# A deformable convolution with routed experts: the four hat spreads as row groups of one array pass, a band ahead of sampling

## The chip, the cores and the metric

One core of a Trainium2 chip runs the whole kernel. The metric is device time in microseconds (us) of one execution, smaller is better. TensorE (PE) multiplies matrices, VectorE (DVE), ScalarE (ACT) and GpSimd (POOL) work element by element, SyncE (SP) issues transfers.

## What is computed

The input is four images of 32 x 32 positions with 128 channels. First a deformable 3 x 3 convolution is added to it, then a top-2 mixture of eight experts:

```python
x = x + _L0_conv_ref(_ln_c(x), w_offset, b_offset, filt)
t = _to_tokens(x)
t = t + _L0_ffn_ref(_ln_t(t), gate_w, gate_b, W1, b1, W2, b2)
# in the convolution, for each position and each of nine taps:
sampled = (v00*(1-dy)*(1-dx) + v01*(1-dy)*dx + v10*dy*(1-dx) + v11*dy*dx) * mask
# in the experts, for each token:
probs = softmax(xf @ gate_w + gate_b); top2_vals, top2_idx = top_k(probs, 2)
out = sum over the two chosen e of top2_vals * (gelu(xf @ W1[e] + b1[e]) @ W2[e] + b2[e])
```

The offsets and the mask of every tap come from an ordinary 3 x 3 convolution of the layer-normalised input.

## The kernel before

The 4096 positions are 32 bands of 128 (four image rows; eight tiles of 4 x 4). Three stages follow each other: the offset convolution for all images (to about 43 us), the band loop (about 50 to 250 us), and the experts on 39 blocks of 256 routed rows (from about 262 us), at whose end results are gathered and added.

In the band loop sampling is a matrix product. For each tile a window of 10 x 10 positions (`xwin`, 100 partitions) is multiplied with a weight matrix `S` of 100 x (9 taps x 16 positions). `S` is the product of a y part and an x part, each a "hat" (one minus the distance, cut at zero) for ten window rows or columns. Per band:

- POOL computes `dist` (`distances`, L570), DVE makes `tent` and `hat` of it (`hats`, L904 to L912), ACT writes its bf16 high part (`hi_part`, L715), POOL the middle and low parts (`split`, L579 to L582), so that `hat3` holds three bf16 parts that sum to the f32 value. A tap takes 60 columns (three parts of 20), a pair of taps 120.
- PE transposes `hat3` pair by pair into bank 4 (`transpose_hats`, five matmuls, L1269), ACT evacuates it to `hatT` (`evacuate_hatT`, L721): 120 rows of 5 x 128 columns.
- PE spreads y and x onto the 100 window cells (`spread_hats`, L1279 y, L1282 x). The constant `spread_sb` has ones where row and cell belong together; a unit u is 512, 512 or 128 columns (`UNITS`: taps 0, 2, 4, 6, then 1, 3, 5, 7, then 8). Each matmul contracts all 120 rows, those of the other tap and axis against zeros. y goes to bank 0 or 1, x to bank 2 or 3.
- ACT copies y (`copy_y`, L729 into `ysp`), DVE multiplies it with x from PSUM into `S` (`multiply`, L923).
- PE samples in three groups of 3, 3 and 2 tiles (`sample`, L1315), ACT evacuates each (`evacuate_samples`, L758 into `samp`), PE projects with the nine filter taps (`project`, L1326, five taps and then four).
- DVE adds the residual and takes statistics (`residual`, L931 to L939), ACT the square root (`std_band`, L765), DVE normalises (`normalise`, L945 and L949 into `xn2`). PE transposes (`transpose_tokens`, L1336), ACT evacuates (L770), PE multiplies with the gate (`gate`, L1340), DVE takes the two largest (`choose`, six links, L960 to L982), PE counts how many tokens of each expert stand before each (`count_places`, L1347 and L1348 into bank 7), DVE turns that into rows (`place_rows`, four links, L991 to L1007).
- POOL copies the normalised band twice into `payload` with its destination (`pack`, L591 and L593) and scatters it by two indirect transfers (`scatter`, L602).

Each engine runs its own list of these calls in a fixed order, `step(b, ...)`, called by `band_loop`: four bands written out, then a loop of four bands a turn, then the rest. Semaphores alone tie the lists together. In step b PE's list is: spread 0 of b, counts of b-3, spread 1 of b, five taps of the projection of b-1 (after `samples_ready(b-1)`), token transpose of b-2, spread 2 of b, four taps, gate of b-2, sample group 0 of b, hat transposes of b+1, sample groups 1 and 2. ACT's: two y copies, tokens, third y copy, samples 0, hatT of b+1, std of b-1, samples 1, high part of b+2, samples 2. DVE's: places of b-3 between the three multiplies of b, then residual of b-1, choose of b-2 and hats of b+2 link by link, then normalise of b-1. POOL's: split of b+2, distances of b+3, scatter of b-3, pack of b-2. `transpose_hats` also waits until the logits of band b-3 have been read from bank 4, `project` until the places of an earlier band have been read from bank 7. Two slots (`par`, b % 2) exist of most tiles.

Before the loop stand band 0's hats and spreads, and a flag `far` (L1030) on which every engine branches (L1352 on PE): offsets above 2 would take a slower gather. After the loop come a count matmul (L1416), the plan of blocks (L1146 to L1167), eight padding writes into `routed` (L366), and the first row load (L496), which waits for scatters and padding.

## Time and profile before

| | |
|---|---|
| median of 3 runs | 403.73 us (402.92 to 405.21) |
| profiled execution | span 400.1 us from the first to the last instruction; its own total is not given |
| PE busy | 315.2 us, 79% of the span |
| PE weight loads | 264.9 us, 66% |
| DVE busy | 227.3 us, 57% |
| ACT busy | 195.6 us, 49% |
| POOL busy | 228.9 us, 57% |
| mean granted TensorE clock | 0.926 |

The span is shorter than a run's time, since start and end of the program lie around it. An engine's busy share is a mean over three stages with different limits, so the loop is to be read by itself: by stage, by what each engine waits for there, and by one band laid out in time. In such a layout the difference of two starts on PE is what an instruction costs the engine, while its shown duration also holds the time until its result is out.

### The profile page before, as it was taken

The page shows a single profiled execution, that of the slowest core. Times are in us where ns is not written, and L with a number is a line of the kernel's source. Part 1 is how long each engine was busy: PE and PEld are TensorE (multiplying, and loading weights), DVE is VectorE, ACT ScalarE, POOL GpSimd, SP SyncE. Part 2 cuts the span into 40 slices and gives each one's busy share as a digit, 9 for nine tenths or more (in the row PEclk, how much of TensorE's full clock was granted, in tenths as well). Part 3 has the DMA queues.
Part 4 walks back from the last instruction along what each step waited for, and adds up shares of the span by engine and source line. Part 5 has one row for each costly group of instructions (what it writes and reads, how often), then busy time and mean ns, then how long its engine had stood idle before and what let it go on. Part 6 is the DMA issues. An engine that isn't in the chain of part 4 may idle for free.

```text
span 400.1 us, 9901 instructions
## 1 busy us (share of the span) xinstructions
PE 315.2 (79%) x2395; PEld 264.9 (66%) x2395; DVE 227.3 (57%) x988; ACT 195.6 (49%) x526; POOL 228.9 (57%) x351
## 2 busy tenths in 40 slices
PE   0999799999999999999999995049989797885000
PEld 0354688888889888898898994038867686774000
DVE  3983257878778787787887876502222122332085
ACT  1253566565565665756656652314444444442063
POOL 4013043777777777777777766204777777777300
PEclk9999899999999999999999999558999999999555
DMA  8958612222222222222222220855777777762298
GB/s 209 274 164 249 265 54 75 89 80 100 78 93 85 82 99 78 90 94 76 98 84 83 95 80 26 145 139 169 223 222 243 230 231 232 227 221 72 82 315 234
DMA packets 52450, 57.88 MB, mean 145 GB/s; under 512 B 6892, under 2 KB 40423, under 8 KB 52424
## 3 DMA queue, kind: packets, MB, share of 16 engines
q1 hardware_dynamic: 45031, 48.16, 39.1%
q0 software_dynamic: 4544, 8.44, 6.6%
q10 hardware_dynamic: 2848, 0.99, 1.4%
q8 instruction: 9, 0.15, 0.2%
q14 instruction: 18, 0.14, 0.1%
HBM read 30.70 MB, written 14.97 MB: 114 GB/s over the span
## 4 chain that ended last, share of the span: by engine, by line
PE 53%; SPq 16%; issue 10%; DMA 6%; ACT 4%; DVE 4%; POOL 2%; ACTq 2%; DVEq 1%; POOLq 0%
PE bank L1326 18%; PE bank L1315 15%; SPq L481 5%; PE bank L1248 5%; SPq L490 4%; SPq L496 3%; DMA wide<-result 2%; PE bank L1279 2%; PE bank L1433 2%; ACT samp L758 2%; PE bank L1269 2%; PE bank L1260 2%; POOL result L658 2%; DMA routed<-padding_sb 1%; DMA result<-y,to 1%
## 5 line engine op out<-in xcount | busy, mean ns | idle before, releaser
L658 POOL DMA_INDIRECT result<-y,to x78 | 76.8, 985 | 43.8 <-DVE to L1191 26.8
L1326 PE MATMUL bank<-filt_sb,samp 128*128 128x128 f32 x576 | 79.3, 283 | 4.1 <-ACT samp L758 2.5
L1326 PEld LDWEIGHTS bank<-filt_sb,samp 128*128 128x128 f32 x576 | 69.1, 191 | 18.1 <-ACT samp L758 14.2
L1315 PE MATMUL bank<-S,xwin 100*128 100x144 f32 x512 | 78.9, 298 | 1.8 <-issue 1.7
L602 POOL DMA_INDIRECT routed<-payload,slot x64 | 63.2, 987 | 18.5 <-issue 13.5
L758 ACT ACTIVATE samp<-bank 128x432 f32<-128x432 f32 (+1 forms) x96 | 46.3, 484 | 52.8 <-PE bank L1315 52.8
L1315 PEld LDWEIGHTS bank<-S,xwin 100*128 100x128 f32 x512 | 67.7, 193 | 2.2 <-issue 2.0
L923 DVE TENSOR_TENSOR S<-ysp,bank 100x512 f32<-100x512 f32 (+1 forms) x96 | 52.5, 550 | 22.9 <-ACT ysp L729 21.8
L1433 PE MATMUL bank<-rowsT,w_blk 128*128 128x256 f32 x156 | 44.4, 408 | 13.3 <-DMA w_blk<-w_all 10.2
L1199 DVE TENSOR_TENSOR y<-bank,w_blk 128x256 f32<-128x256 f32 x39 | 16.6, 425 | 66.0 <-PE bank L1442 64.2
L822 ACT ACTIVATE rowsT<-bank 128x256 f32<-128x256 f32 x39 | 15.0, 384 | 61.0 <-PE bank L1424 61.0
L729 ACT ACTIVATE ysp<-bank 100x512 f32<-100x512 f32 (+1 forms) x96 | 43.6, 494 | 2.4 <-PE bank L1279 1.5
L579 POOL TENSOR_TENSOR rest<-hat 128x180 f32<-128x180 f32 x32 | 17.0, 531 | 47.2 <-ACT hat L715 47.2
L1442 PE MATMUL bank<-w_blk,hid 128*128 128x128 f32 x312 | 42.1, 279 | 0.0
L1433 PEld LDWEIGHTS bank<-rowsT,w_blk 128*128 128x128 f32 x156 | 27.5, 197 | 20.0 <-ACT hid L829 8.0
L1442 PEld LDWEIGHTS bank<-w_blk,hid 128*128 128x128 f32 x312 | 38.8, 195 | 0.3 <-ACT hid L829 0.2
L829 ACT ACTIVATE hid<-bank,w_blk 128x256 f32<-128x256 f32 x78 | 32.6, 473 | 0.6 <-PE bank L1433 0.6
L1279 PE MATMUL bank<-hatT,spread_sb 120*100 120x512 bf16 (+1 forms) x96 | 32.0, 333 | 0.1
L1282 PE MATMUL bank<-hatT,spread_sb 120*100 120x512 bf16 (+1 forms) x96 | 31.2, 325 | 0.8 <-DVE S L923 0.8
L1424 PE MATMUL bank<-ident_sb,rows_in 128*128 128x128 f32 x78 | 15.9, 287 | 15.1 <-DMA rows_in<-routed 15.1
L570 POOL TENSOR_TENSOR dist<-offs,rel_sb 128x180 f32<-128x180 f32 x32 | 16.2, 508 | 19.3 <-issue 10.7
L1424 PEld LDWEIGHTS bank<-ident_sb,rows_in 128*128 128x128 f32 x78 | 11.0, 147 | 20.3 <-DMA rows_in<-routed 15.1
(110 smaller groups left out, 493.1 us busy)
## 6 DMA issues: line engine op xcount, KB each, us to landing
w_blk<-w_all SPq DMA_DIRECT2D x39, 321.0 KB
xwin<-lines SPq DMA_DIRECT2D x64, 120.0 KB
xwin<-lines SPq DMA_DIRECT2D x32, 160.0 KB
rows_in<-routed SPq DMA_DIRECT2D x39, 129.0 KB
wide<-result SPq DMA_DIRECT2D x16, 256.0 KB, 4.8
w_all<-in_experts SPq DMA_DIRECT2D x4, 642.0 KB, 7.4
out_tiles<-res SPq DMA_DIRECT2D x8, 256.0 KB, 4.6
wide<-in_x_rows SPq DMA_DIRECT2D x3, 512.0 KB, 8.6
```

The source lines that it names most:

```text
L602: nc.gpsimd.indirect_dma_start(routed, bass.IndirectOffsetOnAxis(slot[:, par, c2:c2 + 1], 0), payload[:, par, c2, :], None).then_inc((s.sc ...
L658: nc.gpsimd.indirect_dma_start(result, bass.IndirectOffsetOnAxis(to[:, slot, j:j + 1].bitcast(U32), 0), y[:, slot, j, :], None, bounds_che ...
L729: nc.scalar.activation(ysp[:, slot, 0:n], bank[slot][0:Q, 0:n], ACT.Copy).then_inc(s.y_ready, 1)
L758: nc.scalar.activation(sample_view(par, g), bank[5 + (par + g) % 2][:, 0:GROUPS[g] * TAPS * TT].rearrange("c (t k p) -> c t k p", k=TAPS, ...
L829: nc.scalar.activation(hid[:, slot, h, :], bank[RING + slot][:, h * BLOCK:(h + 1) * BLOCK], ACT.Gelu, bias=w_blk[:, slot, HID + h:HID + h ...
L923: nc.vector.tensor_tensor(S[:, par, c0:c0 + n], ysp[:, slot, 0:n], bank[2 + slot][0:Q, 0:n], ALU.mult).then_inc(s.S_ready, 1)
L1279: nc.tensor.matmul(bank[slot][0:Q, 0:n], spread_sb[:, 2 * odd, :], moving, start=True, stop=True).then_inc(s.y_psum, 1)
L1282: nc.tensor.matmul(bank[2 + slot][0:Q, 0:n], spread_sb[:, 2 * odd + 1, :], moving, start=True, stop=True).then_inc(s.x_psum, 1)
L1315: last = nc.tensor.matmul(bank[5 + (par + g) % 2][:, i * TAPS * TT:(i + 1) * TAPS * TT], xwin[:, par, t, :], weights[:, t], start=True, st ...
L1326: last = nc.tensor.matmul(bank[7][:, 0:C], samp[:, par, j, :], filt_sb[:, order[j], :], start=(j == 0), stop=(j == TAPS - 1))
L1433: last = nc.tensor.matmul(bank[RING + slot][:, h * BLOCK:(h + 1) * BLOCK], w_blk[:, slot, h * P:(h + 1) * P], rowsT[:, slot, :], start=Tru ...
L1442: last = nc.tensor.matmul(bank[slot][:, BLOCK + j * C:BLOCK + (j + 1) * C], hid[:, slot, h, j * P:(j + 1) * P], w_blk[:, slot, W_UP + h * ...
```

## The change

- `hat3` gets groups of 32 columns: for each tap and each axis (y, x) three parts of ten and two zeros. A pair of taps is 128 columns, so `hatT` has four row groups: y and x of the even tap, y and x of the odd tap. The constant `spread` is 128 x 100.
- A spread contracts the 30 rows of one group (`spread_taps`). `spread_hats` issues four in a row: y and x of unit 0 and y and x of unit 1, into banks 0 to 3. `spread_last` issues y and x of unit 2 later, when the first banks have been read.
- The spreads of band b+1 are issued in step b, ahead of the samples of b, the last unit behind them, and hat transposes of b+2 at the end. Copies and multiplies move along.
- POOL computes distances four bands ahead, first in its step, then scatters band b-4, then stamps, then splits b+3. DVE's `normalise` writes both copies of the payload itself, into one of four (`QUEUED`) slots, waiting for an older scatter; POOL's `stamp` adds the destination. `transpose_tokens` reads the payload. `xn2` is gone.
- The places are counted into bank 4 from column 384 on (`WHERE`), between sample groups 0 and 1. `project` no longer waits for them; `transpose_hats` does, for an older band.
- Before the loop band 1's transposes and evacuation, band 2's hats and high part, and distances up to band 3 are done ahead of or around the flag. The tail is reordered.

```diff
-            def spread_hats(b, par, u):
-                pe.wait_ge(s.hatT_ready, b + 1)
-                slot, n, odd = (par + u) % 2, UNITS[u], u % 2
-                moving = hatT[:, 4, :] if u == 2 else hatT[:, 0:4, :].rearrange("r i t -> r (i t)")
-                at_least(pe, s.y_ready, b * 3 + u - 1)
-                nc.tensor.matmul(bank[slot][0:Q, 0:n], spread_sb[:, 2 * odd, :], moving,
-                at_least(pe, s.S_ready, b * 3 + u - 1)
-                nc.tensor.matmul(bank[2 + slot][0:Q, 0:n], spread_sb[:, 2 * odd + 1, :], moving,
+            def spread_taps(par, u):
+                slot, n, odd = (par + u) % 2, UNITS[u], u % 2
+                for yx, arrived in ((0, s.y_psum), (1, s.x_psum)):
+                    first = GROUP * (2 * odd + yx)
+                    rows = slice(first, first + PARTS * WIN)
+                    moving = hatT[rows, 4, :] if u == 2 else hatT[rows, 0:4, :].rearrange("r i t -> r (i t)")
+                    nc.tensor.matmul(bank[2 * yx + slot][0:Q, 0:n], spread_sb[rows, :], moving,
+                                     start=True, stop=True).then_inc(arrived, 1)
+            def spread_hats(b, par):
+                pe.wait_ge(s.hatT_ready, b + 1)
+                at_least(pe, s.y_ready, b * 3)
+                at_least(pe, s.S_ready, b * 3)
+                spread_taps(par, 0)
+                spread_taps(par, 1)
+            def spread_last(b, par):
+                pe.wait_ge(s.y_ready, b * 3 + 1)
+                pe.wait_ge(s.S_ready, b * 3 + 1)
+                spread_taps(par, 2)
...
 PE, step b
-                        spread_hats(b, par, 0)
-                        count_places(b - 3, 1 - par)
-                        spread_hats(b, par, 1)
                         samples_ready(b - 1)
                         project(b - 1, 1 - par, range(FIRST_TAPS), ORDER)
+                        pe.wait_ge(s.hatT_ready, b + 2 if not known or b + 2 < BANDS else BANDS)
+                        transpose_tokens(b - 2, (q + 2) % QUEUED)
-                        transpose_tokens(b - 2, par)
-                        spread_hats(b, par, 2)
                         project(b - 1, 1 - par, range(FIRST_TAPS, TAPS), ORDER)
                         gate(b - 2, par)
+                        spread_hats(b + 1, 1 - par)
                     sample(b, par, loads, 0)
-                        transpose_hats(b + 1, 1 - par)
+                        pe.wait_ge(s.route, (b - 2) * 6 + 1)
+                        count_places(b - 3, 1 - par)
                     sample(b, par, loads, 1)
                     sample(b, par, loads, 2)
+                        spread_last(b + 1, 1 - par)
+                        transpose_hats(b + 2, par)
...
 ACT, step b
-                        copy_y(b, par, 0)
-                        copy_y(b, par, 1)
                         evacuate_tokens(b - 2, par)
-                        copy_y(b, par, 2)
+                        copy_y(b + 1, 1 - par, 0)
+                        copy_y(b + 1, 1 - par, 1)
                     evacuate_samples(b, par, 0)
-                        evacuate_hatT(b + 1)
                         std_band(b - 1, 1 - par)
                     evacuate_samples(b, par, 1)
-                        hi_part(b + 2, par)
                     evacuate_samples(b, par, 2)
+                        evacuate_hatT(b + 2)
+                        copy_y(b + 1, 1 - par, 2)
+                        hi_part(b + 3, 1 - par)
...
 POOL, step b
-                        split(b + 2, par)
-                        distances(b + 3, 1 - par)
-                        scatter(b - 3, 1 - par)
-                        pack(b - 2, par)
+                        distances(b + 4, par)
+                        scatter(b - 4, par, q)
+                        stamp(b - 2, (q + 2) % QUEUED)
+                        split(b + 3, 1 - par)
...
 DVE, step b, new order
+                    place_rows(b - 4, par, 1)
+                    hats(b + 3, other, 0)
+                    place_rows(b - 4, par, 2)
+                    hats(b + 3, other, 1)
+                    place_rows(b - 4, par, 3)
+                    hats(b + 3, other, 2)
+                        multiply(b, par, 2)
+                    residual(b - 1, other, 0)
+                    choose(b - 2, par, 0)
+                    residual(b - 1, other, 1)
+                    choose(b - 2, par, 1)
+                    residual(b - 1, other, 2)
+                    choose(b - 2, par, 2)
+                    place_rows(b - 3, other, 0)
+                        multiply(b + 1, other, 0)
+                    choose(b - 2, par, 3)
+                    choose(b - 2, par, 4)
+                        multiply(b + 1, other, 1)
+                    choose(b - 2, par, 5)
+                    normalise(b - 1, other, (q + 3) % QUEUED)
...
 DVE, normalise
-                at_least(dve, s.payload_ready, 2 * (b - 1))
-                nc.vector.tensor_scalar(xn2[:, par, :], x1[:, b, :], mv1[:, par, 0:1], rs1[:, par:par + 1],
+                if not isinstance(b, int) or b >= QUEUED:
+                    dve.wait_ge((s.scat_even, s.scat_odd)[par],
+                                (b // 2 - 1) * 32 if isinstance(b, int) else (b - par) * 16 - 32)
+                nc.vector.tensor_scalar(payload[:, q, :, 0:C], x1[:, b, :].unsqueeze(1).broadcast_to([P, 2, C]),
+                                        mv1[:, par, 0:1], rs1[:, par:par + 1],
```

## Rows read from the trace of the kernel before

**Rows 1.** The page's chain that ended last: share of the span by engine.
```profile
PE 53%; SPq 16%; issue 10%; DMA 6%; ACT 4%; DVE 4%; POOL 2%; ACTq 2%; DVEq 1%; POOLq 0%
```

**Rows 2.** Busy time by stage: us, PE, PEld, DVE, ACT, POOL, PEclk, DMA, GB/s.
```profile
94.00:119.00 25.00, 24.43 (x202) 21.39 (x200) 19.87 (x93) 15.48 (x42) 18.42 (x33) 1.00 0.26 88
```

**Rows 3.** Waits from 94 to 243 us: waiter, released by: total us, times, longest.
```profile
POOL rest L579 <- ACT hat L715: 24.0, 23, 1.1
DVE S L923 <- ACT ysp L729: 15.7, 24, 0.7
```

**Rows 4.** Timeline of PE over one band: start us, duration us, line, tiles, count.
```profile
150.28 1.38 PE L1326 MATMUL bank<-filt_sb,samp 128*128 128x128 f32 x10
151.49 0.27 PE L1336 MATMUL bank<-ident_sb,xn 128*128 128x128 f32 x1
151.60 0.22 PE L1279 MATMUL bank<-hatT,spread_sb 120*100 120x128 bf16 x1
...
151.72 1.11 PE L1326 MATMUL bank<-filt_sb,samp 128*128 128x128 f32 x8
152.66 0.29 PE L1340 MATMUL bank<-gw_sb,xn2T 128*128 128x8 f32 x2
152.81 0.98 PE L1315 MATMUL bank<-S,xwin 100*128 100x144 f32 x6
153.62 0.44 PE L1269 MATMUL bank<-identb_sb,hat 128*120 128x128 bf16 x5
153.91 1.44 PE L1315 MATMUL bank<-S,xwin 100*128 100x144 f32 x10
155.19 0.38 PE L1279 MATMUL bank<-hatT,spread_sb 120*100 120x512 bf16 x1
...
155.62 0.17 PE L1347 MATMUL bank<-both,before_sb 128*128 128x8 bf16 x1
...
155.68 0.40 PE L1279 MATMUL bank<-hatT,spread_sb 120*100 120x512 bf16 x1
...
156.46 1.38 PE L1326 MATMUL bank<-filt_sb,samp 128*128 128x128 f32 x10 [0.17 <-ACT samp L758]
```

**Rows 5.** Timeline of ACT in the same band.
```profile
150.12 1.08 ACT L729 ACTIVATE ysp<-bank 100x512 f32<-100x512 f32 x2
...
153.88 0.53 ACT L758 ACTIVATE samp<-bank 128x432 f32<-128x432 f32 x1 [1.64 <-PE bank L1315]
...
156.00 0.40 ACT L758 ACTIVATE samp<-bank 128x288 f32<-128x288 f32 x1
```

**Rows 6.** Timeline of PE and its weight loads around the second offset convolution.
```profile
21.53 0.27 PE L1260 MATMUL bank<-fold_sb,conv_sb 128*128 128x27 f32 x1
21.73 0.64 PE L1248 MATMUL bank<-xnT,woff_sb 128*32 128x512 f32 x4
22.19 0.13 PEld L1248 LDWEIGHTS bank<-xnT,woff_sb 128*32 128x32 f32 x4 [0.30 <-issue]
22.62 0.13 PEld L1248 LDWEIGHTS bank<-xnT,woff_sb 128*32 128x32 f32 x4 [0.30 <-issue]
...
25.63 0.60 PE L1248 MATMUL bank<-xnT,woff_sb 128*32 128x512 f32 x2
26.16 0.14 PEld L1236 LDWEIGHTS bank<-ident_sb,wide 128*128 128x128 f32 x1 [0.84 <-issue]
```

**Rows 7.** Timeline at both ends of the band loop.
```profile
45.52 1.28 ACT L777 ACT_TABLE_LOAD   x1
...
51.88 1.38 PE L1326 MATMUL bank<-filt_sb,samp 128*128 128x128 f32 x10
...
241.71 2.27 PE L1326 MATMUL bank<-filt_sb,samp 128*128 128x128 f32 x18
```

**Rows 8.** The chain behind the loop, in order of time: start us, us, what.
```profile
256.13 5.79 DMA routed<-padding_sb
```

**Rows 9.** Timeline of POOL: the last scatter.
```profile
252.89 0.96 POOL L602 DMA_INDIRECT routed<-payload,slot  x1 [0.30 <-issue]
```

More of the change, by code:

```diff
@@ L611, in _ @@
             split(1, 1)
+            distances(2, 0)
+            split(2, 0)
+            distances(3, 1)
             pool.wait_ge(s.offs_ready, IMAGES)
@@ L1028, in _ @@
                 multiply(0, 0, u)
+            for link in range(3):
+                hats(2, 0, link)
             dve.wait_ge(s.near_psum, 1)
@@ L1122, in _ @@
                 b = BANDS - 1
[L1123 removed]
+                run(place_rows, b - 3, 0, range(1, 4))
+                residual(b, 1, 0)
                 choose(b - 1, 0, 0)
[L1125 to L1129 removed]
+                residual(b, 1, 1)
+                choose(b - 1, 0, 1)
```

209 lines of the change are left out of this document (104 added, 105 removed).

## The prediction

> **What bounds the kernel now.** I read the page's chain of work first: PE holds 53% of the whole span [rows 1]. The change touches only the band loop (32 bands, from about 50 us to 244 us), so I then took busy time by stage: in 25 us of that loop PE is busy 24.43 us at a granted clock of 1.00, VectorE (DVE) 19.87, POOL 18.42, ACT 15.48 [rows 2]. A band takes 6.18 us: the ten matmuls that open a projection start at 150.28 and again at 156.46 [rows 4]. The waits say how far the others are from mattering: POOL idles 24.0/23 = 1.04 us a band for ACT's hat, DVE 15.7/24 = 0.65 us for ACT's ysp [rows 3]. Last I read one band of PE instruction by instruction, from start to start [rows 4]: projection 1.21, token transpose 0.11, two small spreads 0.12, rest of projection 0.94, gate 0.15, sample group 0 0.81, hat transposes 0.29, sample groups 1 and 2 1.28, big y and x spread 0.43, counts 0.06, big y and x spread 0.43. Sum 5.83. The remaining 0.35 is a stall: PE has nothing from about 156.11 to 156.46, because ACT evacuates the last sample group only at 156.00, for 0.40 us [rows 5]. So a band is PE's work plus the tail of one ACT evacuation.
>
> **The change part by part.**
>
> *Four spreads side by side.* Each big spread streams 512 columns and costs 0.21 to 0.22 us of issue; four in a row are 0.86 [rows 4]. Now each contracts 30 rows in its own group of 32 rows, writing its own bank. The trace has no matmul split by rows, but it has four split by output columns: the offset convolution. There a round of four, each 512 columns in two passes, comes every 22.62 - 22.19 = 0.43 us [rows 6], which is the streaming time of one. So four together at the price of one is shown for columns; I take it for rows. Bounds of the pack: 0.22 (all start at once) to 0.86 (no overlap). What stands in between is the weight loads: each of the four needs its own 100 columns, and a hat transpose, 0.29/5 = 0.058 us, holds one load and one 128-column stream, so a load is at most 0.058, likely 0.04. Three of them ahead of the last stream: 0.22 + 3 x 0.04 = 0.34. I take 0.34.
>
> *Entering and leaving the split array.* Going into the split, the convolution's first start is 0.20 behind the last fold matmul's start (21.53 to 21.73), where otherwise 0.11 separates two such small ones: +0.09. Coming out, the last two convolution matmuls start at 25.63 and stream 0.43, to 26.06; the next weights load only starts at 26.16, with none hidden beneath the stream: +0.10 and a load of 0.04 [rows 6]. So 0.10 in, 0.13 out; bounds 0 (rows may behave otherwise than columns) and 0.2 each. The Trainium skill, "TensorEngine Tiling (Array Packing)", Key Properties, says that changing the tiling mode drains TensorE while changing only the tile doesn't; by that rule the new order pays four times a band, and these rows agree with 0.1 us. The skill's "TensorE: Matmul & The Clock Gate", Part 3, gives 3.07x for four row tiles of K=32 and 512 columns; by it the pack would be an estimated 0.28 us, and the band 0.06 shorter than mine.
>
> *Order on PE.* Between gate and sample group 0 now stand in, pack and out: 0.10 + 0.34 + 0.13 = 0.57. Behind sample group 2 stand the two small spreads (in 0.10, work 0.14, out 0.13) and the five transposes 0.29, together 0.66. Sample group 2 reaches the projection no sooner than 0.26 (ACT started at 153.88, PE's issue of group 0 had ended at 153.62) + 0.40 + 0.06 = 0.72 [rows 4, 5]. So all of that 0.66 is hidden by the evacuation and costs nothing; if ACT's part fell away it would cost 0.66. Sum of the new band: 1.21 + 0.11 + 0.94 + 0.15 + 0.57 + 0.81 + 0.06 + 1.28 + 0.72 = **5.85 us**, 0.33 less than 6.18.
>
> *ACT.* Its order must let the sample evacuations go at once. Two ysp copies take 1.08 [rows 5], from about 0.5 behind the pack's start, so they end 1.6 behind it; group 0 is ready at 0.34 + 0.13 + 0.81 + 0.26 = 1.54. Level, and the short std behind it has half a us before group 1. ACT doesn't bind, by a small margin. Hat evacuation, third ysp copy and hi part now come behind the samples, under the next projection.
>
> *VectorE.* It loses nothing and writes the normalised row twice (256 elements in place of 128). Its 4.91 us a band (19.87/25 x 6.18) becomes 5.05; the steps that now follow each other directly on it (residual, statistics; chosen, both; placed, slot) wait for their own predecessor, +0.2 to +0.5. There is a ring through it: gate, pack, group 0, counts (0.10 + 0.34 + 0.13 + 0.81), then places, three multiplies, rest of choose, normalise, placing and hats, and only then may PE start the next spreads. Taking away residual, statistics and the first choose steps, which lie ahead of the places (about 1.2), leaves 5.05 + 0.4 - 1.2 + 0.2 for the count to land = 4.45, plus 1.38: **5.8**. This is just below PE's 5.85.
>
> *POOL.* It loses the 256-element payload copy and keeps distances, three splits, two scatters and the stamp. It idled 1.04 us a band for ACT [rows 3], so everything it does now, gaps included, is 6.18 - 1.04 = 5.14: under 5.85 even before the copy goes. The new order puts distances and the scatters of the band four back ahead of the split; the split is not late for it, since its hi part comes later too. The new DVE wait for a scatter looks at one issued a whole band earlier: covered.
>
> *Places in bank 4.* The projection no longer waits for the place step; in its stead hat transposes wait for one that is a band older. In the band shown neither held PE up (the projection's releaser is ACT), so nothing is gained, and nothing lost while the counts run between groups 0 and 1: were they late, all of group 1 would be.
>
> *Before the loop.* Hats of band 2 (three DVE steps, about 1.0) now precede the far flag on which every engine branches, and ACT has one more hat evacuation and a hi part, some 1 us, ahead of the 1.28 us table load of 45.52 [rows 7]. That delays the first samples by 1.0 to 2; the spreads of band 1, 0.86, and its copies no longer lie behind sample 0. Net +0.3 (bounds -0.6, +1.5).
>
> *After the loop.* Band 30's slot is written behind band 31's choice, so the last scatters end up to 2 us later. They are covered: the first row load waits for padding writes whose last one lands at 256.13 + 5.79 = 261.92, and the last scatter's issue ended at 253.85, 8 us earlier [rows 8, 9]. The last normalise comes some 0.5 earlier, the padding rows 0.35 later: -0.1.
>
> **Sum.** From the first projection (51.88) to the last (241.71) are 189.8 us for 31 bands [rows 7], the first two and the last shorter since they lack token work or spreads. New: first 5.6, last 5.3, 29 x 5.85 = 169.7, together 180.6: -9.2. With +0.3 and -0.1: -9.0. The profiled execution shows no total of its own but its span, 400.1; the runs' median of 403.73 is 3.6 above it, kept. 403.7 - 9.0 = **394.7 us**.
>
> **Rivals.**
> - *Rows pack cheaply and no drain is seen.* Pack 0.22 to 0.28, switches 0: band 5.5 to 5.6, DVE's ring 5.45. 29 x 5.55 + 10.6 = 171.5: 385.5. For it: switches inside one stream of bf16 may differ from conv's. Against: both edges of every convolution show the gap.
> - *VectorE's ring becomes the bound.* If its self-waits cost 0.2 more than I took, the band is 6.0: 399. For it: 5.85 against 5.8, and no slack. It shows as PE waiting for S before the pack.
> - *Slower: rows don't overlap.* Pack 0.86 with its drains 1.09 between gate and samples, against 0.57: band 6.37; 29 x 6.37 + 11.2 = 195.9, so +6.1 + 0.2: 410. It decides where pack plus drains pass 0.90. For it: no row of the trace has such matmuls. Against: the column split does overlap.
> - *Nothing gained*: an order of waits (ysp copies late, so every sample evacuation late) puts back the 0.33: 403.
>
> **Chances.** Forecast (392 to 397) 0.45, cheap pack 0.17, VectorE's ring 0.20, nothing gained 0.07, slower 0.11. Leaving out the slower case and the far end of the cheap one gives 385 to 404. A measurement here tells about 0.5% (2 us) from no change: faster 0.81, same 0.08, slower 0.11.
>
> **What would show it.** Band starts of the projection 5.85 apart; the four big spread rows starting within 0.15 us; PE weights of sample group 0 starting some 0.1 behind the pack with idle time on PEld; a stall at the projection, still released by ACT's last sample evacuation, of under 0.1. If PE instead waits for DVE ahead of the spreads, the ring has it. The prediction is wrong at its root if the four starts are 0.2 apart, or if sample evacuations start more than 0.3 behind PE's issue.

## The result, and the profile after

The changed kernel runs in 400.37 us (median of 4 runs, 397.23 to 401.61), the kernel before in 403.62 beside it: a ratio of 0.9897, with a 95% interval of 0.9851 to 0.9944. Timed again beside a part of the experiments it gave 397.97 against 403.54, or 0.9854 (0.9825 to 0.9883). The experiments are compared with that second timing. They ran on three chips, on which the kernel before had medians from 403.54 to 404.21, and the changed kernel was timed again on one of them; so between chips it is the ratios that compare, and 0.001 is 0.4 us. The change gained 3.3 us in the first timing and 5.6 in the second, where 9.0 were forecast. The time of 400.37 lies outside the forecast's 392 to 397 and inside the wide range of 385 to 404; of the gain little more than a third came in the first timing and three fifths in the second.

The loop did nearly what was predicted; what was lost lies at its two ends. First the busy time by stage of the changed kernel, with the columns and length of [rows 2]:

```profile
144.00:169.00 25.00, 24.80 (x215) 21.82 (x213) 21.69 (x100) 17.43 (x44) 17.43 (x31) 1.00 0.27 93
```

PE went from 24.43 to 24.80 busy in 25 us, so the stall of [rows 4] is nearly gone. DVE went from 19.87 to 21.69, which is 21.69/25 x 5.84 = 5.07 us a band (5.05 predicted).

One band on PE, laid out in time, which answers to [rows 4]:

```profile
149.97 1.38 PE L1357 MATMUL bank<-filt_sb,samp 128*128 128x128 f32 x10
151.19 0.27 PE L1367 MATMUL bank<-ident_sb,payload 128*128 128x128 f32 x1
151.30 1.06 PE L1357 MATMUL bank<-filt_sb,samp 128*128 128x128 f32 x8
152.19 0.29 PE L1371 MATMUL bank<-gw_sb,xn2T 128*128 128x8 f32 x2
152.41 0.42 PE L1299 MATMUL bank<-hatT,spread_sb 30*100 30x512 bf16 x4
152.76 1.00 PE L1347 MATMUL bank<-S,xwin 100*128 100x144 f32 x6
153.60 0.17 PE L1378 MATMUL bank<-both,before_sb 128*128 128x8 bf16 x1
...
153.66 1.59 PE L1347 MATMUL bank<-S,xwin 100*128 100x144 f32 x10
155.18 0.26 PE L1299 MATMUL bank<-hatT,spread_sb 30*100 30x128 bf16 x2
155.37 0.45 PE L1287 MATMUL bank<-identb_sb,hat 128*128 128x128 bf16 x5
155.81 0.38 PE L1357 MATMUL bank<-filt_sb,samp 128*128 128x128 f32 x1
```

The projection (line 1357) starts at 149.97 and 155.81: 5.84 us a band, with 5.85 predicted. Most bands of the loop take 5.75 to 5.89; three take 6.05 to 6.97, and they come up below. The four big spreads (line 1299) occupy one row of 0.42. Per term, start to start: gate and the way in 0.22, pack and the way out 0.35, group 0 0.84, counts 0.06, groups 1 and 2 with the way into the small spreads 1.52, small spreads 0.19, transposes 0.44.

The waits from 94 to 243 us, which answer to [rows 3] (waiter, releaser, total, times, longest):

```profile
DVE x L932 <- PE bank L1357: 13.6, 26, 2.3
PEld bank L1347 <- issue: 7.3, 24, 1.4
PEld bank L1357 <- ACT samp L757: 2.9, 18, 0.2
PE bank L1347 <- DMA xwin<-lines: 1.6, 3, 1.1
```

DVE no longer waits for ysp but for the projection, 13.6/26 = 0.52 us: it has slack. PE's loader waits for the sample evacuation 0.16 at a time. The last line is new: in three places PE waits for a window transfer, 1.6 us in all, and these are the three long bands.

Now the ends. Before's last fold matmuls and its first two projections, then after's:

```profile
40.77 1.92 PE L1260 MATMUL bank<-fold_sb,conv_sb 128*128 128x27 f32 x16
...
57.42 0.82 PE L1326 MATMUL bank<-filt_sb,samp 128*128 128x128 f32 x5
```

```profile
41.73 1.92 PE L1276 MATMUL bank<-fold_sb,conv_sb 128*128 128x27 f32 x16
...
45.71 0.34 PE L1299 MATMUL bank<-hatT,spread_sb 30*100 30x128 bf16 x2 [1.71 <-DVE S L924]
...
49.96 4.21 PE L1347 MATMUL bank<-S,xwin 100*128 100x144 f32 x16
...
55.22 3.95 PE L1357 MATMUL bank<-filt_sb,samp 128*128 128x128 f32 x18
...
59.45 2.41 PE L1347 MATMUL bank<-S,xwin 100*128 100x144 f32 x16
...
62.37 0.82 PE L1357 MATMUL bank<-filt_sb,samp 128*128 128x128 f32 x5
```

Before: the fold ends at 42.69, projection 0 starts at 51.88 [rows 7], projection 1 at 57.42. After: 43.65, 55.22 and 62.37. The 16 sampling matmuls of band 0 take 4.21 us where band 1's take 2.41, and projection 0 takes 3.95 where [rows 7] has 2.27 for the same 18 at the loop's end. The busy time in stretches of 2 us says why (the columns of [rows 2]; the granted clock is third from the end), before first:

```profile
46.00:48.00 2.00, 1.05 (x6) 1.08 (x7) 0.00 (x0) 1.00 (x2) 0.00 (x0) 0.84 0.27 107
48.00:50.00 2.00, 2.00 (x13) 1.98 (x12) 0.00 (x0) 1.24 (x2) 0.41 (x1) 0.50 0.00 0
50.00:52.00 2.00, 2.00 (x11) 1.47 (x11) 0.95 (x3) 1.35 (x4) 0.49 (x2) 0.81 0.06 16
```

```profile
44.00:46.00 2.00, 0.29 (x3) 0.20 (x4) 1.90 (x6) 1.08 (x2) 0.00 (x0) 0.79 0.95 388
46.00:48.00 2.00, 0.97 (x15) 0.67 (x13) 1.40 (x6) 1.37 (x4) 0.00 (x0) 0.50 0.17 67
48.00:50.00 2.00, 0.64 (x5) 0.23 (x5) 0.00 (x0) 1.93 (x5) 1.88 (x4) 0.50 0.02 4
...
56.00:58.00 2.00, 2.00 (x11) 2.00 (x11) 0.29 (x1) 0.58 (x3) 1.27 (x3) 0.50 0.22 70
58.00:60.00 2.00, 2.00 (x15) 1.65 (x15) 0.58 (x2) 0.45 (x1) 0.71 (x2) 0.79 0.21 82
```

Both kernels lose the clock in the head. Before, it falls within the stretch from 46 to 48, is at its lower level (1.2 of 2.4 GHz, shown as 0.50) from 48 to 50 and is back at about 51: some 3.4 us at the lower level, an estimate from the clock of these stretches. After, it falls within 44 to 46, where PE was busy for 0.29 of 2 us, PE is busy for 0.97 and 0.64 in the two stretches behind, and the clock stays at 0.50 until nearly 59: an estimated 13.7 us.

Last, the chain behind the loop, to be read against [rows 8]:

```profile
245.33 2.28 DMA routed<-payload,slot
247.71 0.41 DVE slot L1010
...
253.58 6.66 DMA routed<-padding_sb
```

A scatter now stands ahead of the last write of `slot`, and the padding writes behind it. The whole difference of the two profiled executions, by marks on PE (the last mark is the first matmul on routed rows, 264.49 before and 262.80 after):

| stretch | predicted | measured |
|---|---|---|
| start to end of fold | 0 | +1.0 |
| end of fold to second projection | +0.4 | +4.0 (14.73 to 18.72) |
| second to last projection, 30 bands | -9.3 | -8.4 (184.29 to 175.85) |
| last projection to first routed rows | -0.1 | +1.8 (22.78 to 24.58) |
| rest | 0 | -0.4 |
| sum | -9.0 | -2.1, from 400.1 to 398.0 |

The table compares two single executions, and the one of the kernel before was a quick one. In every timed execution the total is 1.8 to 1.9 us above the span (here 399.82 and 398.0), so the span of 400.1 stands for a total of about 402.0, an estimate, while the lowest of all timed executions of the kernel before is 402.38 and its median 403.62. The stretches that it shows for the kernel before may thus be up to some 1.7 us shorter than usual together; where, isn't known. Its mean clock, 0.926, is near the upper end of the timed executions (0.916 to 0.930).

The first line is not the change's: the end of fold varied from 42.1 to 44.0 over the experiments that start from the changed kernel, with equal code up to there. Measured from the end of the fold, the second projection of the second timing's profile stands at 61.69 - 43.25 = 18.44, and this distance is used below.

### The profile page after: what moved, and what is told of

It reads as the page before. It is cut to its first block, busy times and chain, and to the rows that moved or that the text cites. A ratio compares the mean times of both kernels' runs of the same rounds, so it can differ in the third digit from the quotient of the medians.

```text
span 398.0 us, 9795 instructions
## 1 busy us (share of the span) xinstructions
PE 310.6 (78%) x2395; PEld 259.8 (65%) x2395; DVE 229.8 (58%) x988; ACT 202.8 (51%) x526; POOL 218.1 (55%) x319
## 4 chain that ended last, share of the span: by engine, by line
PE 55%; DMA 17%; SPq 16%; issue 6%; DVE 2%; POOL 1%; ACT 1%; ACTq 1%; POOLq 0%; DVEq 0%
PE bank L1347 18%; PE bank L1357 15%; DMA xwin<-lines 6%; PE bank L1264 5%; SPq L482 5%; DMA w_blk<-w_all 4%; PE bank L1299 4%; PE bank L1468 3%; SPq L491 3%; SPq L497 3%; PE bank L1287 2%; DMA wide<-result 2%; PE bank L1477 2%; PE bank L1276 2%; DMA fold_sb<-in_fold 2%
## 5 line engine op out<-in xcount | busy, mean ns | idle before, releaser
L1347 PE MATMUL bank<-S,xwin 100*128 100x144 f32 x512 | 80.8, 308 | 1.6 <-DMA xwin<-lines 1.6
L1357 PE MATMUL bank<-filt_sb,samp 128*128 128x128 f32 x576 | 77.8, 285 | 1.1 <-issue 1.0
L1347 PEld LDWEIGHTS bank<-S,xwin 100*128 100x128 f32 x512 | 69.5, 194 | 11.0 <-issue 9.1
L1357 PEld LDWEIGHTS bank<-filt_sb,samp 128*128 128x128 f32 x576 | 70.9, 196 | 5.6 <-ACT samp L757 3.6
L1468 PE MATMUL bank<-rowsT,w_blk 128*128 128x256 f32 x156 | 44.2, 407 | 14.9 <-DMA w_blk<-w_all 13.7
L757 ACT ACTIVATE samp<-bank 128x432 f32<-128x432 f32 (+1 forms) x96 | 47.1, 491 | 10.6 <-PE bank L1347 6.5
L1299 PE MATMUL bank<-hatT,spread_sb 30*100 30x512 bf16 (+1 forms) x192 | 22.2, 366 | 4.4 <-issue 2.7
L1459 PEld LDWEIGHTS bank<-ident_sb,rows_in 128*128 128x128 f32 x78 | 11.1, 147 | 22.1 <-DMA rows_in<-routed 17.7
L720 ACT ACTIVATE hatT<-bank 128x640 bf16<-128x640 bf16 x32 | 22.5, 704 | 4.6 <-PE bank L1287 2.4
```

The costliest lines, as they stand in the source:

```text
L757: nc.scalar.activation(sample_view(par, g), bank[5 + (par + g) % 2][:, 0:GROUPS[g] * TAPS * TT].rearrange("c (t k p) -> c t k p", k=TAPS, ...
L1299: nc.tensor.matmul(bank[2 * yx + slot][0:Q, 0:n], spread_sb[rows, :], moving, start=True, stop=True).then_inc(arrived, 1)
L1347: last = nc.tensor.matmul(bank[5 + (par + g) % 2][:, i * TAPS * TT:(i + 1) * TAPS * TT], xwin[:, par, t, :], weights[:, t], start=True, st ...
L1357: last = nc.tensor.matmul(bank[7][:, 0:C], samp[:, par, j, :], filt_sb[:, order[j], :], start=(j == 0), stop=(j == TAPS - 1))
L1459: last = nc.tensor.transpose(bank[slot][:, j * P:(j + 1) * P], rows_in[:, slot, j, 0:C], ident_sb[:, :])
L1468: last = nc.tensor.matmul(bank[RING + slot][:, h * BLOCK:(h + 1) * BLOCK], w_blk[:, slot, h * P:(h + 1) * P], rowsT[:, slot, :], start=Tru ...
```

## The experiments

Two questions: was the loop's gain what I took it for (rows packed, stall hidden), and what took 4 us ahead of it and 1.8 behind it.

### All 128 rows, no packing

```diff
-                    moving = hatT[rows, 4, :] if u == 2 ...
-                    nc.tensor.matmul(bank[2 * yx + slot][0:Q, 0:n], spread_sb[rows, :], moving,
+                    moving = hatT[:, 4, :] if u == 2 ...
+                    nc.tensor.matmul(bank[2 * yx + slot][0:Q, 0:n], spread_sb[:, at:at + Q], moving,
```

> The changed kernel with every spread contracting all 128 rows again (its weights zero outside its group of 32), so no two can run side by side and the array is never split; order and waits are those of the change. Theory (the loop's gain comes from packing, four for 0.35 us in place of 0.86 plus switches): the step from the first spread to sample group 0 becomes 0.86, the band 5.84 + 0.86 - 0.35 - 0.07 = 6.28 at most, 6.14 if PE alone sets it; total 8 to 12 us above the changed kernel, thus above the kernel before. Rival (the gain comes from moving the spreads out of the stretch between sampling and projection, and packing matters little): band under 6.0, total within 4 us of the changed kernel.

408.71 us, ratio 1.0121 (1.0093 to 1.015): 10.7 over the changed kernel, as expected, and slower than the kernel before.

```profile
150.59 1.04 PE L1301 MATMUL bank<-hatT,spread_sb 128*100 128x512 bf16 x4 [0.17 <-issue]
151.46 0.90 PE L1349 MATMUL bank<-S,xwin 100*128 100x144 f32 x6
```

The four spreads hold PE 151.46 - 150.59 = 0.87 against 0.35, and a band, from gate to gate (150.13 to 156.46), is 6.33 (6.23 in the mean of 30 bands). All that the order gains is less than what four spreads cost when they no longer hide behind an evacuation: the packing carries the gain.

### The kernel before with row groups alone, y and x as a pair

```diff
-SLOT = PARTS * HATS
+GROUP = 32
+SLOT = 2 * GROUP
...
-                nc.tensor.matmul(bank[slot][0:Q, 0:n], spread_sb[:, 2 * odd, :], moving,
+                for yx, arrived in ((0, s.y_psum), (1, s.x_psum)):
+                    nc.tensor.matmul(bank[2 * yx + slot][0:Q, 0:n], spread_sb[rows, :], moving,
```

> The kernel before with the row groups alone: y and x of a unit side by side (three packs of two a band), its order, waits and payload copies untouched. Theory (each entry into a split array costs 0.1 and each way out 0.13, about what a pack of two saves): big packs 0.26 + 0.23 against 0.43, the small one 0.12 + 0.23 against 0.12, of which the stall of 0.35 ahead of the projection hides the two big ones: band 6.2 to 6.35, total 0 to 5 us above the kernel before. Rival (switching is nearly free for rows): band under 6.1 only if the stall moves too; PE's stall grows by 0.3 and the total stays within 1 us.

413.77, ratio 1.0247 (1.0219 to 1.0275).

```profile
156.34 0.42 PE L1283 MATMUL bank<-hatT,spread_sb 30*100 30x512 bf16 x2
156.69 0.18 PE L1348 MATMUL bank<-both,before_sb 128*128 128x8 bf16 x1
...
157.46 0.71 PE L1327 MATMUL bank<-filt_sb,samp 128*128 128x128 f32 x4 [0.23 <-ACT samp L758]
```

A pair costs 156.69 - 156.34 = 0.35, as much as the pack of four, against 0.43 unsplit, and it is paid twice; between the projection's two halves the small pair takes 0.19, where [rows 4] has 0.12 for both. The sign was expected, the size was not: +10 us. The band of 6.34 that is shown here is the shortest of every four in the loop; the others take 6.57 to 6.66, and from the second projection to the last a band takes 193.68/30 = 6.46 us in the mean, against 184.29/30 = 6.14 before. Most of that is waiting ahead of the projection. From 94 to 243 us:

```profile
PE bank L1327 <- ACT samp L758: 6.3, 16, 0.5
PE bank L1327 <- DVE place L991: 2.7, 5, 0.5
```

PE waits 6.3 + 2.7 = 9.0 us there, and the kernel before 1.8 + 1.1 = 2.9 for the same two: a quarter of a microsecond a band more. In the band shown the two big pairs save 0.08 each, but the small one gives 0.07 back, and what stands ahead of each pair takes longer to the next start (token transpose 0.20 for 0.11, rest of the projection 1.00 for 0.94, sample groups 1 and 2 1.38 for 1.28). So row groups alone, in the old places, lose, by the changes of mode and by a longer stall. Why the stall grows was not followed up, and pairs in the new order were not run: this doesn't show that two at a time can never pay.

### The small spreads back over full rows

```diff
+                    if u == 2:
+                        rows = slice(0, 2 * SLOT)
```

> The changed kernel with the two small spreads behind the samples over all 128 rows (no split of the array there; weights zero outside their group), the four big ones packed as before. The prediction put the two switches of this place (0.23 us) at nothing, since the last sample evacuation covers them: total within 0.7 us of the changed kernel, the stall ahead of the projection 0.1 to 0.2 longer. Rival (they are on the path): 0.1 to 0.2 a band, 3 to 6 us lower.

397.22, ratio 0.9828 (0.9794 to 0.9862), against the changed kernel's 0.9854: the two intervals overlap.

```profile
150.63 1.38 PE L1361 MATMUL bank<-filt_sb,samp 128*128 128x128 f32 x10
...
156.47 0.71 PE L1361 MATMUL bank<-filt_sb,samp 128*128 128x128 f32 x4 [0.17 <-ACT samp L758]
```

The band stays at 5.84 (5.97 in one of four), the wait for ACT returns (0.17): the two changes of mode behind the samples lie under the evacuation, as the sum had them.

### One more VectorE copy a band

```diff
+                    nc.vector.tensor_copy(gsum[:, 0:4, :], filt_sb[:, 0:4, :])
                     normalise(b - 1, other, (q + 3) % QUEUED)
```

> The changed kernel with one more VectorE instruction a band, a copy of 512 elements into a tile nobody uses, ahead of normalise: 0.3 to 0.6 us of VectorE time. The prediction's ring through VectorE was 5.8 us against PE's 5.85: by it the band grows by the copy less 0.05, and the total by 8 to 16 us. Rival (the ring was overpriced: VectorE still waits 13.6/26 = 0.52 us a band for the projection in the changed kernel): the wait shrinks by the copy, the band stays below 5.95, total within 3 us.

406.54, ratio 1.0058 (1.0034 to 1.0082), about 8 us over the changed kernel by the ratios, within what was expected.

```profile
150.90 0.42 PE L1300 MATMUL bank<-hatT,spread_sb 30*100 30x512 bf16 x4 [0.44 <-issue]
```

The band (gate at 150.17 and 156.43) grows by 0.42, what the copy takes: PE waits 0.44 ahead of the pack. That holds for three bands of four in the loop (6.19 to 6.33); the fourth stays at 5.84. So the ring through VectorE is real, and in three bands of four it is within some hundredths of PE's own period; in the fourth it has at least 0.4 to spare.

### Window transfers cut to 3/10 (a part of the windows isn't loaded, so part of the sampling is left out)

```diff
+                    if not isinstance(b, int) or b >= 2:
+                        w1 = w0 + 1
```

> The changed kernel with each window load from band 2 on cut to one window column of its part (3 of 10 columns, so 120 KB a band in place of 400 KB; stale data stand in the rest, so that part of the sampling is left out). Theory (the windows now land just at the time they are needed, and three or four times in the loop later): the PE waits for windows (1.6 us in the trace of the changed kernel) vanish, every band 5.84, total 1.5 us lower. Rival 1 (transfers held the bands up all through): bands fall below 5.80 and the total by over 3 us. Rival 2: nothing moves.

397.83, ratio 0.9837 (0.9816 to 0.9858), against 0.9854. The wait of PE for `xwin` is gone from the list, no band between the second and the last projection takes over 5.84, and the 30 bands take 174.2 us in place of 175.5 and 175.9 in the two profiles of the changed kernel. The transfers take 7.3 to 8.2 us each where they stand on the chain. So the windows cost 1.3 to 1.7 us of the loop in the traces; the total moved by 0.7, which the intervals don't tell from nothing, nor from the 1.5 that were expected.

### Four places for the slots

```diff
-            slot = sb("slot", [P, 2, 2], U32)
+            slot = sb("slot", [P, QUEUED, 2], U32)
```

> The changed kernel with four places for the slot numbers in place of two, and in the four bands of the tail a wait for the scatter two bands older. Theory (behind the loop VectorE's last slot write waits 0.98 us for a scatter's landing, and the padding rows are queued behind it on VectorE): that wait is gone, the padding writes start 1 us earlier and the first row block arrives 1 us earlier: 1.0 us below the changed kernel. Rival (the padding writes then share the DMA queues with the last scatters and land later, as they took 6.66 us here against 5.79 before): under 0.4 us gained.

398.04, ratio 0.9855 (0.9831 to 0.988).

```profile
250.15 7.06 DMA routed<-padding_sb
```

The scatter is gone from the chain, but the last padding write took 7.06 us to land, 6.66 in the changed kernel's profile and 5.79 before. The total shows no gain. The tail itself, from the last projection to the first matmul on routed rows, does: it is 22.9 to 23.5 us in the six profiles with four places for the slots (they follow below) and 23.8 to 24.6 in eight with two, the changed kernel's own two among them. So the wait was real and worth under a microsecond; the other half of the tail's 1.8 is the landing, in which padding writes and late scatters are under way together. Whether these scatters slow it was not tested.

### The far flag earlier

```diff
             spread_hats(0, 0)
+            (near counts of the flag)
             spread_last(0, 0)
             transpose_hats(1, 1)
...
+            (flag)
             for u in range(3):
                 multiply(0, 0, u)
```

> The changed kernel with the far flag written ahead of band 0's multiplies and band 2's hats (as early as the near counts allow), ScalarE's masks and table load ahead of the extra hat evacuation, all else the same. Theory A (the gain was lost ahead of the loop, because every engine branches on a flag that now comes 2 us later and VectorE needs 4.8 us from the flag to its first loop step, 47.64 to 52.39): flag near 45.5, first projection near 53.1 in place of 55.12, total 2 us below the changed kernel (about 398.3). Rival B (the flag is not what the first projection waits for; the half TensorE clock between 46 and 59 us is): first projection and total stay within 0.7 us of the changed kernel.

398.27, ratio 0.9833 (0.9802 to 0.9864). The flag came at 45.21 in place of 47.50, but the first projection at 54.65 and not at 53.1, and of the expected 2 us the ratio shows less than 1, within the intervals:

```profile
49.34 0.67 PE L1299 MATMUL bank<-hatT,spread_sb 30*100 30x512 bf16 x4 [2.62 <-ACT hatT L720]
...
54.65 2.27 PE L1357 MATMUL bank<-filt_sb,samp 128*128 128x128 f32 x18
```

In this kernel ACT's evacuation of band 1's hats had come behind the table load of [rows 7], so the wait for the flag became a wait for that. Yet projection 0 ran in 2.27: here the clock had fallen later, within 46 to 48, and was back at 54. From the fold's end it is 16.7 to projection 1, not 18.4. That the median doesn't follow says how much one profiled start differs from the next.

### Idle matmuls ahead of the loop

```diff
+            for _ in range(3):
+                nc.tensor.matmul(bank[7][:, :], ident_sb[:, :], filt_sb[:, 0:4, :]..., start=True, stop=True)
...
+            for _ in range(5): (the same, after transpose_hats(1, 1))
```

> The changed kernel with eight idle f32 matmuls of 512 columns on PE ahead of the loop (three behind the first spreads, five behind the near counts) into a bank not yet in use, so that PE isn't idle there; the flag stays late. Theory: the granted clock stays at 1.00 where it was 0.50 from 46 to 59 us, so samples 0 (4.14 us at the low clock, about 2.4 at the full one) and projection 0 (3.74 against 2.2) give back 1.5 to 3 us of the first bands; the second projection starts near 60 in place of 62.44. Rival: VectorE's late entry into the loop sets the first band and the clock costs nothing (within 0.5 us of the changed kernel), or the filler delays the near counts and the flag and it is slower by up to 1 us.

397.13, ratio 0.9822 (0.9802 to 0.9841).

```profile
46.20 4.56 PE L1340 MATMUL bank<-filt_sb,ident_sb 128*128 128x512 f32 x10
51.04 2.41 PE L1354 MATMUL bank<-S,xwin 100*128 100x144 f32 x16
...
54.61 2.23 PE L1364 MATMUL bank<-filt_sb,samp 128*128 128x128 f32 x18
```

The granted clock is 1.00 in every stretch from 46 to 60, and samples and projection take 2.41 and 2.23. But the row itself was too long, 4.56 us: the loop's first pack starts 50.69 - 42.30 = 8.4 behind the fold's end, in the changed kernel 49.36 - 43.65 = 5.7, and the second projection 60.03 - 42.30 = 17.7, not 18.4. A part of what the clock gave back went there. By the ratios the total is 1.3 us lower, and the intervals overlap; the pair of kernels at the end of this section is the one that prices the clock.

### Flag, idle matmuls and slots together

> The changed kernel with the early flag, the idle matmuls ahead of the loop and the four slot places together. If the three losses at the ends are separate, the gains add up: flag 2.1, clock 3.2, tail 2.3 by the first looks, 5 to 7 us below the changed kernel (393.5 to 395.5), 0.975 of the kernel before. If flag and clock are one loss seen twice (filling the wait or shortening it), 3.5 to 5 us.

396.28, ratio 0.9818 (0.979 to 0.9847): no more than the idle matmuls gave, within the intervals, where 3.5 to 7 us below the changed kernel were expected and 1.7 came. Projection 0 starts at 54.63 again.

### Another order at the head, with and without idle matmuls

Flag early, evacuation of band 1's hats ahead of the masks, distances of band 3 ahead of the split, four slots; 3 + 1 idle matmuls, and none.

> The changed kernel with all causes of the late first band treated at once: far flag first, ScalarE evacuates band 1's hats ahead of masks and table load (in the early-flag run PE waited for just this evacuation, queued behind the table load), POOL computes distances of band 3 ahead of the split of band 2 (VectorE's first loop step waited for them there), idle matmuls only as long as the gap (1.3 us and 0.9 us, since those of the run before were 4.5 us long by themselves), and the four slot places. Theory (the head's loss is a chain of several queues, each of which takes over when one is removed): first projection at 52 to 53 in place of 54.6, second near 57.8 to 58.5 in place of 60.1; total 1.5 to 3 us below the run with all three single remedies (396.3). Rival (VectorE's own way from the flag into the loop, 4.8 us, sets it): first projection stays above 54.

> The same as the run with the rearranged head, without the idle matmuls. Theory (the low clock costs by itself): the granted clock falls to 0.50 near 46 us, samples 0 take 4.1 us in place of 2.4, and the first projection comes 1 to 1.7 us later than with them; total 1 to 2 us higher. Rival (VectorE's entry into the loop hides it): equal within 0.5 us.

398.93, ratio 0.9881 (0.9857 to 0.9905), and 397.49, ratio 0.9854 (0.983 to 0.9877). Both missed. With idle matmuls the flag stood behind them (47.17 in place of 44.70), VectorE entered the loop at 53.73, PE was busy for 0.76 and 0.56 in the stretches 52 to 54 and 54 to 56, and the clock fell to 0.50 all the same. Without them VectorE entered at 51.60, 6.9 behind a flag at 44.70. So the flag was not what held it.

### Masks first; then all repairs, with and without idle matmuls

```diff
             copy_y(0, 0, 0)
             copy_y(0, 0, 1)
+            for m in range(1, IMAGES):
+                mask_image(m)
             copy_y(0, 0, 2)
...
             distances(2, 0)
+            distances(3, 1)
             split(2, 0)
```

> The changed kernel with one move ahead of the loop: ScalarE's three remaining image masks come before its copies of the hats, and the distances of band 3 before the split of band 2. Theory (VectorE enters its loop about 4 us after the last image mask, and the first placing, and so the first loading of projections, hangs on it): VectorE's first loop step starts at 49.5 to 50.5 instead of 52.4; TensorE's first projection starts at 54 to 54.6 instead of 55.2, because the samples of band 0 at a granted clock of 0.50 end there anyway; total 0.3 to 1 us under the changed kernel's 398, at 397 to 397.7. Rival (the entry hangs on the far flag, not on the masks): VectorE's first step stays at 51.5 or later, time unchanged.

> All the repairs together: image masks first, far flag early, distances of band 3 early, a short row of idle matmuls (two of 512 float32 columns) ahead of the loop, four slot places. Theory (the head lost 3 to 5 us to late masks and to a granted clock of 0.50 in bands 0 and 1): VectorE's first step at about 49.3, first projection at 52 to 53 and 2.2 us long, second at 57.5 to 58.5; total 393.5 to 395. Rival (the first projection is held by the samples of band 0 and their evacuation, whatever comes before): first projection at 54 or later, total 396 to 397, as the kernel with flag, idle matmuls and slots.

> The same without the idle matmuls, to price the clock in the head by itself. Theory: first projection at 53 to 54 and 3.7 us long at a granted clock of 0.50, second at 59.5 to 60.5; total 1 to 2.5 us above the kernel with idle matmuls. Rival (the idle matmuls delay as much as the clock gives back): both within 0.5 us of one another.

Masks first: 397.94, ratio 0.9852 (0.9821 to 0.9883), no change. VectorE's first step in the loop came at 50.36, which from the fold's end is 8.15 against 52.09 - 43.25 = 8.84 in the changed kernel's second profile, but PE's samples, at a clock of 0.50, ended later than that anyway; from the fold's end the second projection stands at 60.77 - 42.21 = 18.56. All repairs: 395.11, ratio 0.9791 (0.9766 to 0.9817), the fastest of all and the only one whose interval lies wholly below the changed kernel's. The same without idle matmuls: 397.51, ratio 0.9848 (0.9827 to 0.9868). With them, PE and the clock:

```profile
51.76 0.76 PE L1360 MATMUL bank<-S,xwin 100*128 100x144 f32 x4 [1.29 <-ACT samp L757]
...
54.21 2.23 PE L1370 MATMUL bank<-filt_sb,samp 128*128 128x128 f32 x18
```

```profile
52.00:54.00 2.00, 0.78 (x8) 0.53 (x8) 1.91 (x5) 0.54 (x2) 0.51 (x1) 1.00 0.02 4
```

Without them:

```profile
48.62 4.21 PE L1354 MATMUL bank<-S,xwin 100*128 100x144 f32 x16
...
54.46 4.16 PE L1364 MATMUL bank<-filt_sb,samp 128*128 128x128 f32 x18
```

From the fold's end to the second projection 59.64 - 43.96 = 15.7 with, 61.81 - 43.39 = 18.4 without, 14.7 in the kernel before. The two kernels differ in nothing but two idle matmuls of 1.1 us each: the lower clock costs 2.7 us in these profiles and 397.51 - 395.11 = 2.4 in the medians. The expected first projection at 52 to 53 was missed, at 54.21. What holds it there is VectorE:

```profile
52.02 0.35 DVE L906 SCALAR_TENSOR_TENSOR tent<-dist 128x180 f32<-128x180 f32 x1 [3.61 <-issue]
...
52.95 1.28 DVE L925 TENSOR_TENSOR S<-ysp,bank 100x512 f32<-100x512 f32 x2
```

```profile
53.73 0.26 PE L1305 MATMUL bank<-hatT,spread_sb 30*100 30x128 bf16 x2 [1.22 <-issue]
```

PE's small spreads, which stand ahead of the projection, wait until VectorE has multiplied the first unit of band 1, and they start at 53.73. VectorE's hats of band 2, ahead of the branch, end at 48.41; its first step behind the branch starts 3.61 later. Without the idle matmuls it is 3.94, with the masks alone 4.17. In the changed kernel it is 4.76 behind the flag, but there VectorE also waits ahead of the branch for ScalarE's masks, which end at 48.44, 3.95 before its first step. The flag at 45.76 had long been there. So nearly 4 us pass on VectorE between the last thing that it does or waits for ahead of the branch and its first step behind it, and the hats of band 2 push that forward. That the hats would be cheaper behind the branch follows from these numbers but was not run.

Why it takes so long was not tested either. One candidate is in the traces: the transfers on the queues that the profile calls instruction. The changed kernel has 27 packets on them in all, and these between 45 and 55 us (queue, packets, MB, share):

```profile
q14 instruction: 5, 0.04, 1.6%
```

The five lie between 49.5 and 53.5, while the 50 us from 100 to 150 have one; the kernel before has five between 47.0 and 50.5. No run separated this from other causes.

## Why the prediction was right and wrong

**The bound and the band: right.** 5.84 a band against 5.85, PE the bound, the sample stall nearly gone, DVE 5.07 against 5.05. The band without packing shows that the mechanism is the one named.

**Inside the band, two errors of 0.15 cancel.** From gate to group 0 the sum had 0.15 + 0.57 = 0.72 and the trace has 152.76 - 152.19 = 0.57: pack and way out are 0.35, not 0.34 + 0.13, while the way in took 0.07 and not 0.10. From group 1 to the next projection it had 1.28 + 0.72 = 2.00, and the trace has 155.81 - 153.66 = 2.15, because the groups with the way into the small spreads take 1.52, and spreads and transposes 0.63 behind them. That the sum hits to 0.01 is luck; its terms are good to 0.15. The Trainium skill, "TensorE: Matmul & The Clock Gate", Part 3, gives a gain of 3.07x for four row tiles; this kernel shows 0.87/0.35 = 2.5x with the way out counted in, so the measured number stands.

**Row groups may be taken from column groups: right.** The loader idles ahead of group 0, (7.3 - 1.4)/23 = 0.26 us a band without the longest, and that idle is inside the 0.35.

**VectorE's ring at 5.8: right for three bands of four.** It doesn't bind, and 0.42 more on it moves these bands by 0.42; the fourth has room for it.

**The loop: 30 bands gained 8.4 in place of 9.3.** The three waits for windows, 1.6 us, are more than this difference, and the prediction didn't name window transfers at all. With the windows cut the 30 bands gain 184.3 - 174.2 = 10.1, so without this wait the sum would have come out too small by 0.8.

**Before the loop: the step that failed.** The prediction opens with the change touching only the band loop, and for the head it had +0.3, with +1.5 as its far end; measured are 4.0 up to the second projection, between two single executions of which the one before was quick. It counted the instructions that were added ahead of the branch, but not two things that hang on them. One is TensorE's clock: the prediction read it only in the loop, where it is 1.00, although the head's stretches were in the same trace, with 0.50 from 48 to 50. The clock falls within 44 to 46 in the changed kernel, ahead of the flag: PE idles 1.71 us there where it idled 0.77 before, since the packed spreads are done sooner and the small ones wait for VectorE's multiply as they did (they start 2.06 behind the fold's end, 2.02 before). The delayed start behind it leaves PE at 0.97 and 0.64 busy in the next two stretches, and the lower clock then holds for samples and projection of band 0. That is 2.4 us by the pair with and without idle matmuls; which part of it is due to the earlier fall and which to the later start was not separated. The other is VectorE's entry into the loop, 52.39 against 50.13: before, it waited for POOL's distances, which stand behind the branch too and started at 49.59, 4.1 behind the flag; now band 2's hats, hi part and masks stand ahead of its branch. With the clock repaired, 15.7 - 14.7 = 1.0 us is left, and in that trace PE waits for VectorE's first multiply of the loop ahead of projection 0, so this is taken to be it; no kernel was run with VectorE's entry repaired.

**Behind the loop: wrong in one wait.** I had priced the late scatters against the padding's landing and found them covered. They are, for the row load. But `slot` has two places, and its last write waits for the scatter of the band two older: 0.98 us ahead of the padding. The padding's landing, 6.66 against 5.79, made up the rest.

**The level: a term misread.** The prediction kept 3.6 us between the span of 400.1 and the time. Every timed execution shows 1.8 to 1.9; the other 1.7 is that the profiled execution was quicker than the median. In a forecast that is the median less a difference the error falls out, but the head of that quick execution is what the changed one's was measured against.

**The rivals.** No overlap is excluded by the band without packing, cheap pack and VectorE's ring by the band of 5.84. None of the cases had the loss where it was: all five priced the steady band and took the head from one count of instructions.

## What to carry to other kernels

When a change moves work of the first iterations ahead of a branch or a loop, price the head like the loop: engine by engine up to the second period, with the granted clock of each stretch: here the pauses ahead of the loop were paid at half speed for over ten microseconds. Small matmuls on row groups paid here with four in a row behind one change of mode; pairs in the old places lost 10 us. When a kernel's loop gets faster, look for what was just in time before: here the window transfers held three bands up. When an array has fewer places than a queue is deep, its last writes inherit the queue's wait: follow each buffer to the end of the kernel.

## What the runs showed of the hardware

- Four matmuls of 30 rows, 100 output partitions and 512 bf16 columns, each in its own row group and bank: 0.35 us from the first's start to the next instruction's, way out included. Two: 0.35 as well. Four over 128 rows: 0.87.
- With PE resuming work at 49.3, the granted clock was back at 54 in one kernel and near 59 in another with almost the same work between; the second projection stood 16.7 and 18.7 behind the fold's end. The kernel with the longer row of idle matmuls had its 5 runs within 0.9 us, the changed kernel its 6 within 2.8; but the one with all repairs, at a clock of 1.00 too, had its 5 within 3.0.
- Between VectorE's last step ahead of a branch on a flag and its first one behind it passed 3.6 to 4.2 us in five kernels in which the trace names no other cause, and 4.76 in the changed kernel, 3.95 behind the masks that it waited for. PE, whose near counts end at 46.97 there, starts its loop at 49.36, 2.4 later.
- 512 columns of float32 against 128 x 128 weights are two matmul instructions of about 0.45 each.
